# A four-stage transformer kernel: one maximum for four heads in the two 16-wide attentions, the causal mask as products on TensorE, and the routed experts' activation split on VectorE

## The reference

```
a: causal attention, 16 heads of width 16, with biases
b: 32 experts with a squared relu, 6 of them weighted per token, plus a shared one
c: attention of 16 heads without a mask: softmax(q1 k1 s - lam q2 k2 s), q1, q2 of width 8, v of width 16
d: causal attention, 16 query heads of width 128 on 4 key heads; then
e: 2 of 8 experts per token, y = (silu(h w1) * (h w3)) w2, hidden width 896
```

## Time and profile before

| | us |
|---|---|
| median of 3 runs | 2582.18 (2580.67 to 2585.19) |
| the profiled execution's own time | 2578.62 |
| its span, first to last instruction | 2576.6 |
| PE busy in the span | 1992.0 (77%) |
| DVE busy | 1651.5 (64%) |
| ACT busy | 1194.4 (46%) |
| POOL busy | 894.5 (35%) |

### The profile page before, as it was taken

One profiled execution on the slowest core, in us unless ns is written; L12 is line 12 of the kernel. 1 busy time (PEld: TensorE's weight loads), 2 busy tenths in 40 slices (PEclk: granted clock), 3 DMA queues, 4 the chain that ended last, 5 costly groups with the idle time before them and its releaser, 6 DMA issues. The chain is left out here.

```text
span 2576.6 us, 41368 instructions
## 1 busy us (share of the span) xinstructions
PE 1992.0 (77%) x12002; PEld 1510.7 (59%) x12002; DVE 1651.5 (64%) x3889; ACT 1194.4 (46%) x2360; POOL 894.5 (35%) x962
## 2 busy tenths in 40 slices
PE   7388875499999574788577769999979509999980
PEld 4233344499999441333355547777769509999980
DVE  5444436788888765786678767777754416666654
ACT  1143331244444221666245458888853116666650
POOL 0122222255555301000145544444420144444445
PEclk9555566699999785999789889999989659999995
DMA  4211100000000032220122222222254245555523
GB/s 148 82 51 51 50 8 1 33 25 24 22 19 16 9 143 58 56 63 26 69 82 98 98 105 100 106 93 98 102 180 147 94 162 194 203 203 203 200 71 98
DMA packets 92993, 231.32 MB, mean 90 GB/s; under 512 B 13424, under 2 KB 38896, under 8 KB 85744
## 3 DMA queue, kind: packets, MB, share of 16 engines
q1 hardware_dynamic: 89840, 221.96, 24.4%
q0 software_dynamic: 3072, 8.39, 1.0%
HBM read 156.91 MB, written 72.88 MB: 89 GB/s over the span
## 5 line engine op out<-in xcount | busy, mean ns | idle before, releaser
L2078 POOL TENSOR_TENSOR e_moe_act_low<-e_moe_act,e_moe_act_high 128x256 fp32r<-128x256 f32 x161 | 180.1, 1124 | 223.5 <-ACT e_moe_act_high L2046 223.5
L539 POOL TENSOR_SCALAR d_att_probs<-d_att_probs,d_att_rinv 128x128 f32<-128x128 f32 (+2 forms) x192 | 177.6, 925 | 216.8 <-DVE d_att_rinv L550 216.8
L1434 DVE SCALAR_TENSOR_TENSOR b_acc<-bank,b_gates,b_acc 128x256 f32<-128x256 f32 x512 | 212.4, 478 | 41.8 <-PE bank L1349 41.8
L1402 POOL TENSOR_TENSOR b_moe_act_low<-b_moe_act,b_moe_act_high 128x512 fp32r<-128x512 f32 x136 | 176.2, 1295 | 177.4 <-ACT b_moe_act_high L1379 177.4
L901 DVE CUSTOM_DVE_ANT_0 a_att_masked<-bank,a_att_lower 128x128 f32<-128x128 f32 (+3 forms) x256 | 116.9, 490 | 137.5 <-PE bank L699 133.6
L904 DVE TENSOR_REDUCE c_att_rmax<-bank 128x1 f32<-128x512 f32 x256 | 164.9, 686 | 56.8 <-PE bank L699 51.7
L429 PE MATMUL wide<-d_att_k,d_att_q 128*128 128x128 f32 (+3 forms) x512 | 186.5, 447 | 17.8 <-DMA d_att_k<-k_dram 17.7
L2011 PE MATMUL wide<-e_moe_hT_high,e_moe_w_high 128*128 128x256 f32 x644 | 183.4, 285 | 13.0 <-DVE e_moe_w_low L2088 13.0
L2011 PE MATMUL wide<-e_moe_hT_low,e_moe_w_high 128*128 128x256 f32 x644 | 183.1, 284 | 0.0
L2011 PE MATMUL wide<-e_moe_hT_high,e_moe_w_low 128*128 128x256 f32 x644 | 183.1, 284 | 0.0
L2088 DVE TENSOR_TENSOR e_moe_w_low<-e_moe_w,e_moe_w_high 128x768 fp32r<-128x768 f32 x161 | 153.8, 958 | 31.4 <-ACT e_moe_w_high L2040 12.1
(11 more groups left out here) (360 smaller groups left out, 5973.9 us busy)
## 6 DMA issues: line engine op xcount, KB each, us to landing
e_moe_w<-in_e_w SPq DMA_DIRECT2D x23, 2688.0 KB, 10.2
q_dram<-d_in_rot SPq DMA_DIRECT2D x16, 1024.0 KB, 3.9
d_att_q<-q_dram SPq DMA_DIRECT2D x16, 1024.0 KB, 5.0
o_dram<-d_att_o SPq DMA_DIRECT2D x64, 256.0 KB, 2.0
d_out_oT<-o_dram SPq DMA_DIRECT2D x16, 1024.0 KB, 5.6
b_moe_w<-in_b_w SPq DMA_DIRECT2D x17, 512.0 KB, 3.3
a_att_q<-q_parts SPq DMA_DIRECT2D x96, 64.0 KB, 2.2
a_att_k<-k_parts SPq DMA_DIRECT2D x96, 64.0 KB, 2.2
```

The lines of the kernel that those rows point to most:

```text
L539: g.tensor_scalar(tile, tile, rinv[:, j, qt:qt + 1], None, ALU.mult).then_inc(scaled, 1)
L1402: g.tensor_tensor(ap[1][:, u % 4, :], act[:, u % 4, :], ap[0][:, u % 4, :], ALU.subtract).then_inc(act_low, 1)
L1434: nc.vector.scalar_tensor_tensor(out=tile, in0=y, scalar=gate, in1=tile, op0=ALU.mult, op1=ALU.add).then_inc(acc_done, 1)
L2078: g.tensor_tensor(ap[1][:, f, :], act[:, f % 4, :], ap[0][:, f, :], ALU.subtract).then_inc(act_low, 1)
```

## The change

Constant rows of `qs` and `ks` (now made in the stage, not in the attention) are filled by GpSimd in the projection, behind the root of each sequence. In the attention the row scores of all four heads of a step go into banks 0 to 3 (one buffer), and VectorE takes one reduction over the four banks with the sign turned (`negate`). The column scores go through the ring of three banks instead, one bank per head, with one exponential per head. In a the mask is added by two further products of 64 columns per head on the diagonal tile, from two constant tables of 64 rows per half (`pick`, `never`), which are loaded and cast at the start. SP loads q of groups 0 and 1 and the tables first; ScalarE's queue loads k of groups 0 and 1. In the swiglu blocks VectorE makes the low part of the activation; a block starts when five of the seven weight chunks are split (they hold all of w1 and w3), and chunks 5 and 6 are split at the end of the block.

```diff
-                with g.Fori(0, B) as b:
+                for b in range(B):
                     norm.root(g, b)
+                    g.wait_ge(norm.root_done, b + 1)
+                    for r in (32, 96):
+                        g.memset(qs[b][r:r + 32, :, :].bitcast(F32), 0.0).then_inc(constant, 1)
+                        g.memset(ks[b][r:r + 32, :, :].bitcast(F32), 1.0).then_inc(constant, 1)
+                    g.wait_ge(constant, 4 * b + 4)
...
-        cpair = [[c.bank[2 * s + g] for g in range(2)] for s in range(2)]
-        cwide = c.wide
-        rbank, obank = c.bank[4:7], c.bank[7]
...
+        rpair = [c.wide[:, 2 * s:2 * s + 2, :] for s in range(2)]
+        cbank, obank = c.bank[4:7], c.bank[7]
...
-        def place(qt, slot, g):
-
-            r = 4 * qt + 2 * slot + g
-            return r + (qt > 1) + (qt > 2)
+        def place(kt, hq):
+
+            r = 4 * ((kt - 1) % NQ) + hq
+            return r + (kt == 3) + 2 * (kt == 0)
...
-                sp.wait_ge(zeroed, 8)
-                sp.wait_ge(ones_ready, 8)
-                for s in range(4):
+                load_half(sp, qs[0], q_parts, (0, 0, 1), 0, 0)
+                load_half(sp, qs[1], q_parts, (0, 0, 1), 1, 1)
+                if causal:
+                    sp.dma_start(raw_pick[:, :, :], mask["pick"]).then_inc(mask_in, 16)
+                    sp.dma_start(raw_cut[:, :, :], mask["never"]).then_inc(mask_in, 16)
+                for s in range(2, 4):
                     load_quad(s, s)
...
-                def rows(n, s, qt, slot, turned, divided):
-
+                def rows(n, s, qt, slot, first):
+
+                    if slot == 0 and not (first and qt == 0):
+                        pe.wait_ge(max_ready, 4 * n + qt)
+                    w = keys(qt)
...
+                        mm = nc.tensor.matmul(rpair[slot][:, g, 0:w], half(qs[s], g, ROWS)[:, slot, qt * P:(qt + 1) * P],
+                                              half(ks[s], g, ROWS)[:, slot, 0:w], start=True, stop=not causal)
+                        if not causal:
+                            mm.then_inc(rows_done, 1)
+                    if causal:
+                        for i in range(2):
+                            for g in range(2):
+                                lo = w - P + PAIR * i
+                                mm = nc.tensor.matmul(rpair[slot][:, g, lo:lo + PAIR], half(pick, g, PAIR)[:, i, :], half(never, g, PAIR)[:, i, :],
+                                                      start=False, stop=(i == 1))
+                                if i == 1:
+                                    mm.then_inc(rows_done, 1)
+
...
+                def ring_free(n, at, first, following):
+
+                    j = at - 3
+                    if j == TM_AT:
+                        if following:
+                            pe.wait_ge(mT_ready, n + 2)
+                    elif j == TQ_AT:
+                        if not first:
+                            pe.wait_ge(o_ready, n)
+                    else:
+                        pe.wait_ge(exp_done, 16 * n + (5 + j - (j > TM_AT) - (j > TQ_AT)))
 
...
-                            pe.wait_ge(exp_done, 8 * n + 2 * kt + slot + 1)
+                            if kt < NQ - 1 or following:
+                                for g in range(2):
+                                    ring_free(n, place((kt + 1) % NQ, 2 * slot + g), first, following)
                             if kt < NQ - 1:
-                                cols(n, b, s, kt + 1, slot)
+                                cols(b, s, kt + 1, slot)
                             elif following:
-                                cols(n + 1, nb, ns, 0, slot)
-                            if ahead:
-                                if kt == 0 and slot == 0:
+                                cols(nb, ns, 0, slot)
+                            if ahead and slot == 0:
+                                if kt == 0:
                                     pe.wait_ge(loaded[rs], 192 * rb + 192)
...
-                        for slot in range(2):
-                            a.wait_ge(cols_done, 16 * n + 4 * kt + 2 * slot + 2)
-                            nc.scalar.activation(probs[kt % 2][:, 2 * slot:2 * slot + 2, lo:S], cwide[:, 2 * slot:2 * slot + 2, lo:S],
-                                                 ACT.Exp).then_inc(exp_done, 1)
+                        for hq in range(4):
+                            if hq % 2 == 0:
+                                a.wait_ge(cols_done, 16 * n + 4 * kt + hq + 2)
+                            nc.scalar.activation(probs[kt % 2][:, hq, lo:S], cbank[place(kt, hq) % 3][:, lo:S], ACT.Exp).then_inc(exp_done, 1)
...
+                load_half(a, ks[0], k_parts, (0, 1, 0), 0, 0)
+                load_half(a, ks[1], k_parts, (0, 1, 0), 1, 1)
...
-                def maxima(n, s, qt, slot, g, reused):
-                    r = 4 * qt + 2 * slot + g
-                    if r == 0 and reused:
+                def maxima(n, s, qt, reused):
+                    if qt == 0 and reused:
                         v.wait_ge(split, 2 * n - 2)
-                    if g == 0:
-                        v.wait_ge(rows_done, 16 * n + r + 2)
-                    w, hq = keys(qt), 2 * slot + g
-                    dst, bank = rmax[s % 2][:, qt, hq:hq + 1], rbank[place(qt, slot, g) % 3]
-                    if causal:
-                        if reused or n or qt:
-                            v.wait_ge(max_ready, 16 * n + (r - 3))
-                        hold(v, carry)
-                        nc.vector.tensor_tensor_reduce(masked[:, r % 4, 0:w], bank[:, 0:w], lower[:, S - w:S], 1.0, -3e38, ALU.add, ALU.max,
-                                                       dst).then_inc(max_ready, 1)
-                    else:
-                        nc.vector.tensor_reduce(dst, bank[:, 0:w], AX.X, ALU.max).then_inc(max_ready, 1)
+                    v.wait_ge(rows_done, 16 * n + 4 * qt + 4)
+                    nc.vector.tensor_reduce(rmax[s % 2][:, qt, :], c.wide[:, :, 0:keys(qt)], AX.X, ALU.max,
+                                            negate=True).then_inc(max_ready, 1)
...
-                    pe.wait_ge(w_low, FC1 * j + FC1)
+                    pe.wait_ge(w_low, FC1 * j + EARLY)
...
+                    pe.wait_ge(w_low, FC1 * j + FC1)
...
-                        if following:
+                        if f:
+                            high_act(j, f - 1)
+                        if following and f < EARLY:
                             if f == 0:
                                 a.wait_ge(w_in[1 - s], 16 * (m + s) + 16)
                                 a.wait_ge(y_done, j)
                             high_weights(1 - s, f)
-                        if f:
-                            high_act(j, f - 1)
                     high_act(j, FC1 - 1)
                     if following:
                         keep_hT(j + 1, 1 - s)
+                        for f in range(EARLY, FC1):
+                            high_weights(1 - s, f)
...
-            @block.gpsimd
-            def _(g):
-                def low_act(j, f):
-                    g.wait_ge(act_high, FC1 * j + (f + 1))
-                    g.tensor_tensor(ap[1][:, f, :], act[:, f % 4, :], ap[0][:, f, :], ALU.subtract).then_inc(act_low, 1)
-
-                with g.Fori(0, BLOCKS) as j:
-                    for f in range(FC1):
-                        low_act(j, f)
...
+                def low_act(j, f):
+                    v.wait_ge(act_high, FC1 * j + (f + 1))
+                    nc.vector.tensor_tensor(ap[1][:, f, :], act[:, f % 4, :], ap[0][:, f, :], ALU.subtract).then_inc(act_low, 1)
...
-                        if following:
+                        if f:
+                            low_act(j, f - 1)
+                        if following and f < EARLY:
                             low_weights(j + 1, 1 - s, f)
+                    low_act(j, FC1 - 1)
                     if following:
                         low_hT(j + 1, 1 - s)
+                        for f in range(EARLY, FC1):
+                            low_weights(j + 1, 1 - s, f)
...
+    pick = np.stack([r[None, :] == h[:, None],
+                     (r[None, :] - P // 2 == h[:, None]) & (r[None, :] < P - 1) | (r[None, :] < P // 2) & (h[:, None] == P // 2 - 1)], axis=1)
+    above = h[None, :] > h[:, None]
+    never = np.stack([above, above | (h[:, None] == P // 2 - 1)], axis=1)
```

More of the change, by code:

```diff
@@ L582, in _, with narrow_attention @@
                     step(7, j, False, True)
-def narrow_attention(c, name, q_parts, k_parts, vals, out, causal):
+def narrow_attention(c, name, q_parts, k_parts, qs, ks, vals, out, mask):
     nc = c.nc
@@ L596, in narrow_attention @@
     PAIR, ROWS = 64, 48
+    causal = mask is not None
     def keys(qt):
@@ L609, in sem @@
             return c.sem(f"{name}_{n}")
-        qs = [sb(f"q{s}", [P, 2, S], F32R) for s in range(4)]
-        ks = [sb(f"k{s}", [P, 2, S], F32R) for s in range(4)]
```

(40 more changed lines are left out.)

98 lines of the change are left out of this document (52 added, 46 removed).

## The result

| | us |
|---|---|
| before, median | 2581.43 (2579.61 to 2585.19) |
| changed, median | 2554.85 (2547.56 to 2555.39) |
| ratio | 0.9889, 95% interval 0.9868 to 0.9910 |
| forecast | 2512 (2470 to 2545) |
| profiled execution, its span | 2554.9, 2552.9 |

The kernel gained 27 us where 70 were forecast, and the time lies outside the range. These are the stretches of the earlier trace rows after the change, with the ends of both attentions as third and fifth row. The columns are those of the earlier trace rows.

A forecast was written before the change was run, and what follows sets the result against it. TensorE was taken to bound both attention loops and swiglu, its waits being winnable. a -24.8, c -18.8, swiglu -27, single-head starts +1: together -70, giving a median of 2512 us, range 2470 to 2545.

The forecast's parts named there:

- Swiglu: Swiglu blocks: TensorE's waits for GpSimd's low half vanish, -25.3 us over 22 blocks; first block starts earlier, -1.7; together -27.
- c: the total: Second narrow attention: start -12.2 us, loop of 14 groups -6.6 at 13.1 us a group, together -18.8.
- a, masks: Loop of a: four mask pairs per step add 0.37 us, 1.5 us a group (0.8 to 2.6).
- a, first row scores, -3: Start of a: row scores of the first two groups take 20.4 us instead of 23.66, -3 (0 to -3.5).
- a, waits removed: Loop of a: of 3.94 us of TensorE waits a group before second row-score pairs, 3.5 us goes.
- a, start: Start of a: mask tables land some 2.3 us after issue and are cast by 86.3 instead of 94.08, -7.8 us.
- Projection, "nothing": Projection: GpSimd's 16 memsets of 0.99 us beside VectorE and TensorE work cost nothing.
- A: Rival: the clock rises in a, a group takes about 11.6 us instead of 15.6, -56 us to 2456; chance 0.14.
- B: Rival: the clock falls in c because the single buffer breaks TensorE's work into bursts, +62 us to 2574; chance 0.04.
- D: Rival: VectorE is late in swiglu and TensorE waits as before, +25 us to 2537; chance 0.10.
- E: Rival: slower, TensorE and VectorE alternate over the four banks without overlap in both loops, about 2695 us; chance 0.05.
- C: Rival: both attention loops gain nothing, masks at 0.16 and the single buffer eat the gains, +21 us to 2533; chance 0.18.

The follow-up runs named there:

- e3: Changed kernel without mask products and tables in a, row maxima taken over masked keys too: 2503.45 us, ratio 0.9703.
- e4: Changed kernel with the two mask table loads issued ahead of the q loads of a: 2548.03 us, ratio 0.9868.
- e5: Changed kernel with GpSimd's constants of each sequence behind VectorE's four normalisations of that sequence instead of beside them: 2553.12 us, ratio 0.9894.
- e15: Changed kernel with column scores of groups 14 and 15 in banks 0 to 3, one per head, instead of the ring of three: 2546.44 us, ratio 0.9861.
- e17: Changed kernel without masks, constants behind the normalisations, a's row and column scores 512 wide, four banks for the last two groups' column scores: 2481.90 us, ratio 0.9609.
- e14: Changed kernel without masks, constants behind the normalisations, plus later groups' loads held until earlier ones have landed: 2502.34 us against 2502.03 without the holding.

## Why the prediction was wrong, step by step

*Swiglu: right in mechanism and size.* -27 forecast, -28.0 measured, of which 1.6 is the earlier first block (1.7 forecast); a block at 15.49, and in the waits view of twenty-one blocks no wait is left, where GpSimd's low half had cost 11.9 us.

*c: the total right in part by luck.* The start gave 8.4 instead of 12.2: the second queue was taken to save 2.7 us, but the loads landed after 6.2 to 6.9 us instead of 2.2, and the first rows came 1.1 later after the first issue than before. The loop gave 0.76 a group instead of 0.47: the chain of a step is the one worked out, with a release of 0.05 to 0.15 instead of 0.17, pairs and hand-over of 0.80 to 0.84 as counted, and a reduction of 2.29. 2.9 us went in the end, which had been priced at nothing. Three misses of opposite signs, 3.8 short at the start, 4 over in the loop and 2.9 short at the end, left 17.1 of 18.8. One of the signs of being wrong did come: in each of the twelve groups TensorE waits for the DMA of the transposed maxima. It costs 0.37 a group, so this chain is the next limit, as the prediction feared, and single exponentials are not quite free either.

```profile
PE bank L736 <- DMA c_q<-c_att_mT: 4.4, 12, 0.4
PE bank L736 <- ACT c_att_probs L830: 3.4, 12, 0.4
```

*a, masks: the failed step.* "So I take 0.11 for three of the four pairs of a step and 0.05 for the last: 0.37 a step, 1.5 us a group". Measured 5.46 - 2.88 = 2.6, the upper bound, or 2.2 by groups with 3.20. The 0.11 is the time from a load's start to its products' start (160.77 to 160.88), not the time until the next load can start; and the 512 columns of 165.74 are a row in which the next load is hidden. In the short step nothing hides it: three pairs in 0.64 us (243.63 to 244.27) are 0.213 a pair. The Trainium skill, "TensorE: Matmul & The Clock Gate", "LDWEIGHTS (loading the stationary operand)", says that a load's time goes by its columns and not by its rows. The trace agrees as far as it goes: loads of 48 and of 64 rows, all of 128 columns, keep the same pace of 0.214. An estimate by that page's figure, 128 / 1.2 = 107 ns a load, gives 0.213 for the two loads of a pair if they go one after the other.

*a, first row scores, -3.* Measured 0. Without mask products (e3) the time to the first copy falls from 17.98 to 13.6, so the masks took 4.4 us here, 2.2 a group where 1.5 was counted; that is about half of the miss, and the rest was not traced.

*a, waits removed.* "Of the 3.94 us about 0.11 each is the weight load ... so 3.5 us goes". This is the second failed step. The four figures of the earlier trace rows are idle time of the weight loads (PEld), and products still run while no load does. The products (PE) of the same places in the same group waited 0.67, 0.20, 0.62 and 0.86, together 2.35; two of them:

```profile
150.76 0.80 PE L699 MATMUL bank<-a_att_k,a_att_q 48*128 48x512 f32 x2 [0.67 <-DVE a_att_rmax L901]
162.47 0.69 PE L699 MATMUL bank<-a_att_k,a_att_q 48*128 48x384 f32 x2 [0.86 <-DVE a_att_rmax L901]
```

The twelve groups say the same: 29.1/12 = 2.4, and so do, (198.97 - 169.92)/12 = 2.4. The new stall, 1.1 forecast, is 0.43 (5.2/12), and 0.17 went to two other waits. So waits gave 1.8 instead of 2.4, masks and the blocks around them took 2.2 instead of 1.5, and the loop lost 0.4 us a group instead of gaining 1.0.

*a, start.* "land some 2.3 us later": 8.9 us, behind 24 loads issued just before on two queues; e4 gives the price, 7.4 us in the trace.

*Projection, "nothing".* The cover was there for time, not for the data path: VectorE's first four normalisations start at 15.68, the memsets at 15.70, and four take 4.23 us instead of 1.38. In c the four are as slow, but its projection took only 0.2 us more. The Trainium skill, "SBUF — State Buffer", "Who interferes with whom", names this: a copy, cast or `tensor_scalar` of VectorE in a two-port mode and a GpSimd operation take one port pair in turn, each for its whole length. The trace agrees: one normalisation per memset, 1.12 us beside 0.94 to 1.09, and in the later sequences only a normalisation that begins during a memset is slow (0.8 us, one of four); e5 takes it away. It was a rule that spoke against the change, and it was not weighed.

*Ends, "the row block stands in between".* Not in the last two groups, where nothing is computed ahead: +5.6 in a, +2.9 in c, for the most part by the ring (e15, e17).

*Rivals.* A was wrong for the change (clock 0.52 with TensorE busy 96%). The rise it named can happen, and a group at clock 1.00 then takes the 11.6 us that it counted, but no denser loop brought it here: with no masks the clock rises at times, with wide products to 0.86. By the rule quoted there a denser loop should rise; the densest by busy share, with 96%, did not. The premise, too, was read too quickly: c, the loop with the high clock, was busy 130.89/162.65 = 80%, a 85%. B, D and E did not come: c kept 1.00, and no wait is left in swiglu. C (2533) named the masks at their upper bound, but kept the starts' gains, which also failed.

## What to carry to other kernels

Price a short product by its weight load, not by its stream, and read that load in a place where no long stream covers it. Read what TensorE waits from its products, not from its weight loads, whose idle time also holds products that still stream. When single terms of a sum miss in opposite ways, the total proves none of them. For work moved beside other work, ask which port, queue and bank it shares, and walk through the first and last rounds of a loop, where the covering work is missing.

## What the runs showed of the hardware that was not expected

- Two products of 64 rows and 128 weight columns in the two row halves take 0.213 us at 1.2 GHz when nothing covers their loads (243.13 to 244.20); a row block takes the same 5.46 us whether they stream 16 or 64 columns.
- Loads of 64 KB issued from two queues at once land after 6.2 to 6.9 us instead of 2.2, at 129 GB/s instead of 125; with 12 let go at a time they land after 3.5 to 3.8 (e14).
- GpSimd's memsets of 32x1024 slow VectorE's fp32 normalisations of 128x256 from 0.41 to 1.12 us each where each meets a memset, to 0.8 where it begins during one, and not at all where they do not overlap (e5).
- A loop with TensorE busy 96% was granted 0.52; one with no mask products and all scores 512 wide, 85% busy, was granted 0.86. Making the scores wide, 3072 columns more for TensorE to stream in each group of four heads (two heads at once), saved 13 us (2502.03 to 2489.24).
